# First attention of a two-layer block: four heads per group of value products, and a new order of the neighbouring work

## The chip, the cores and the metric

The kernel runs on one core of a Trainium2 chip. Its engines work side by side, each through its own list of instructions, and wait for each other on semaphores: TensorE (PE in the profile; PEld are its weight loads), VectorE (DVE), ScalarE (ACT), GpSimd (POOL) and SyncE (SP), which here issues most DMAs. The metric is the device time of one execution in microseconds (us), lower is better.

## What is computed

Two transformer layers over x of 32 sequences x 256 tokens x 128 channels, 16 heads of 8 channels, all float32 at the border. Cut to what the change touches, the first layer's attention:

```python
h = layernorm(x) * (1 + ca) + sa
Q, K, V = proj(Wq, bq), proj(Wk, bk), proj(Wv, bv)        # h @ W.T + b, split in 16 heads of 8
Qn = Q / maximum(norm(Q), 1e-12);  Kn = K / maximum(norm(K), 1e-12)
attn = softmax(Qn @ Kn.T / sqrt(8))                        # 256 x 256 per head and sequence
x = x + ga * ((attn @ V) * gate @ Wo.T + bo)
h = layernorm(x) * (1 + cb) + sb                           # goes to the first layer's experts
logits, depth = h @ gate_w + gate_b, h @ dp_w1 + dp_b1     # the router's products
```

After it come the four dense experts of layer 0, the causal attention of layer 1, and eight routed experts of layer 1.

## The kernel before

The program is a chain of phases with a barrier of all engines between them. The change lies in the first phase alone, in the functions named `dense` of each engine. They run over the 32 sequences (here: batches, `b`), one batch at a time, as a pipeline in which every engine works on several batches at once. No scheduler sets the order: each engine's loop over `b` is written out by hand, and an instruction starts when all ahead of it on its engine have started and its semaphores have come.

What belongs to batch b:

- `project` (PE): two products of 128 tokens each give Q, K and V in the PSUM tile `M` (`M[:,0]` for the first half of the tokens, `M[:,1]` for the second). `take` (DVE) adds the bias and stores them, one instruction for each half.
- `square` (ACT), `lengths` (DVE) and `lengths` (POOL, a Newton iteration of three rounds) give the inverse norms; `unit` (DVE) scales Q and K. `high` (ACT) and `low` (DVE) split them in float16 halves; four transposing DMAs on SP (`turned`) bring them to `qs3` and `ksd`.
- The 16 heads go in eight chunks `u` of two heads (CH = 8). `score` (PE) makes the 256 x 256 scores of both heads in a PSUM tile `SP[u % 2]`; `exp` (ACT) writes the exponentials to `pt[:, u % 4]`; `values` (PE) multiplies them with V. A head's V has 8 columns and a column of ones, padded to 32, so that a head uses 32 of the array's 128 columns: `tile_position=(0, 32 * g)` for head g of a group of four. The products are in float32, four instructions in a chunk (two halves of the keys, two heads).
- `tail_t(b, 0)` and `tail_t(b, 1)` (DVE) turn the first and the second half of `OP` into `oT`; `tail_n` divides by the sums and ends in `aT`; `tail_wo` (PE) multiplies with Wo; `tail_w`, `tail_g` and `tail_x` (DVE) add it to x; `tile_stats` and, every second batch, `variance` give the statistics of the next norm; `deviation` (POOL) finishes them for two batches.
- For the second norm: `normal` (ACT) writes z, `turn` (PE) transposes it into `M[:, 0]`, `enter` (ACT) modulates it into `hcur` and `h16`, `low` (POOL) makes the low half, `router` (PE) multiplies it into `M[:, 1]`, `extra` (DVE) takes that out of PSUM, `depth` (DVE) uses it.

In the loop for batch b PE issues score(b, u) and then values of two chunks earlier. Behind the chunks stand project(b + 3), both halves, at u = 1; tail_wo(b - 1) at u = 4; turn(b - 3) at u = 5; router(b - 3) at u = 7. ACT issues the eight exp, with high(b + 2) behind the third, square(b + 3) and normal(b - 3) behind the fifth, enter(b - 3) behind the seventh. The waits that matter below: exp(u) waits for score(u); score(u) for exp(u - 2), whose PSUM tile it writes; `take` for `project`, half by half; `lengths` (DVE) for `square`; `unit` for `lengths` of POOL; `high` for `unit`; `tail_w` for `tail_wo`; `project` for the `enter` and `extra` that emptied its half of `M` last.

## Time and profile before

| | us |
|---|---|
| median of 3 runs | 1810.16 (1807.91 to 1816.59) |
| the profiled execution | 1828.18 |
| its span | 1826.0 |
| PE busy over the span | 1556.5 (85%) |
| DVE busy | 1284.0 (70%) |
| ACT busy | 1188.8 (65%) |
| POOL busy | 882.6 (48%) |
| the stage of the change, from its first to its last exp | 81.4 to 524.5 |

The profiled execution is one run, some 18 us above the median; all rows below are from it. Starts are counted from the span's start. In the timeline a row is a run of like instructions of one engine: when it began, how long until its last record ends, the engine, the line of the kernel, output and inputs with their shapes, how many (x), and in brackets how long the engine had stood idle just before, with the instruction of another engine that ended the wait. Neighbouring instructions of one engine overlap by about a tenth of a microsecond, so that the distance of two starts, not the length of a row, is what a step costs its engine. One float32 product on PE stands as two records in the trace.

### The profile page before, as it was taken

What the parts mean: (1) busy time and instruction counts of PE and PEld (TensorE: products, weight loads), DVE (VectorE), ACT (ScalarE), POOL (GpSimd) and SP (SyncE); (2) the same over time, 40 slices, a digit from 0 to 9 for tenths busy, and PEclk for the clock granted to TensorE, in tenths of its full rate; (3) what the DMA queues carried; (4) which work ended last, traced back from release to release, by engine and by line L of the source; (5) the groups of instructions that cost most, each with busy time, mean ns of one, the idle gap of its engine ahead of it and who ended that gap; (6) DMA issues with size and microseconds to landing.
All of it is one profiled execution on the core that took longest, in us unless ns stands there. A gap on an engine that the chain in (4) does not pass through costs nothing.

```text
span 1826.0 us, 39932 instructions
## 1 busy us (share of the span) xinstructions
PE 1556.5 (85%) x12803; PEld 796.7 (44%) x12803; DVE 1284.0 (70%) x3451; ACT 1188.8 (65%) x2134; POOL 882.6 (48%) x1677
## 2 busy tenths in 40 slices
PE   5799999999967999779999999999999508989970
PEld 3334444444433444324444444444444306777750
DVE  6566777777747888836767677675877536777768
ACT  3777788778756989635565665556555517888860
POOL 6254544545511333324444438747465563555554
PEclk9899999999988999969999999999999558999995
DMA  5221112221208930022211213312221323222228
GB/s 155 75 45 36 36 36 41 42 37 36 47 13 331 386 125 1 23 57 50 48 41 41 46 38 66 69 43 66 45 62 43 112 77 97 75 77 76 76 66 258
DMA packets 238478, 141.20 MB, mean 77 GB/s; under 512 B 184163, under 2 KB 210659, under 8 KB 237253
## 3 DMA queue, kind: packets, MB, share of 16 engines
q1 hardware_dynamic: 227072, 119.72, 24.4%
q0 software_dynamic: 8640, 17.97, 3.0%
q8 instruction: 108, 1.77, 0.4%
q10 hardware_dynamic: 2564, 0.97, 0.2%
q14 instruction: 94, 0.76, 0.1%
HBM read 37.67 MB, written 58.98 MB: 53 GB/s over the span
## 4 chain that ended last, share of the span: by engine, by line
PE 42%; DVE 12%; issue 6%; ACT 2%; DVEq 2%; POOL 2%; DMA 1%; POOLq 1%; SPq 0%; ACTq 0%; another core or an unknown queue 0%
PE OP L2138 8%; PE OP L2003 5%; PE M L2101 5%; PE SP L1983 4%; DVE mx L1329 4%; PE SP L2298 3%; PE SP L2118 2%; PE M L2076 2%; PE M L2097 2%; PE M L2092 2%; PE OP L2313 2%; DVE pt L1620 2%; POOL h_dram L492 1%; PE OP L2150 1%; PE M L1993 1%
## 5 line engine op out<-in xcount | busy, mean ns | idle before, releaser
L863 ACT ACTIVATE pt<-SP 128x768 f32<-128x768 f32 x256 | 207.1, 809 | 250.4 <-PE SP L2118 236.4
L1329 DVE TENSOR_REDUCE mx<-M 128x2 f32<-128x512 f32 (+1 forms) x384 | 258.0, 683 | 104.5 <-PE M L2101 94.6
L531 POOL TENSOR_SCALAR_AFFINE_SELECT pt<-pt 128x256 f32<-128x256 f32 x512 | 198.6, 412 | 262.8 <-ACT pt L863 260.9
L750 ACT ACTIVATE pt<-SP 128x1024 f32<-128x1024 f32 x256 | 255.2, 1019 | 72.1 <-PE SP L1873 72.0
L562 POOL DMA_INDIRECT y_dram<-hT,dest x142 | 140.2, 987 | 134.2 <-DVE hT L1626 112.0
L964 ACT ACTIVATE pt<-SP,b 128x256 f16<-128x256 f32 x284 | 138.2, 487 | 81.8 <-PE SP L2298 81.2
L1892 PE MATMUL OP<-pt,vs 128*32 128x256 f32 x1408 | 186.5, 387 | 0.0
L492 POOL DMA_INDIRECT h_dram<-hT,slot x128 | 130.7, 1021 | 58.8 <-issue 31.7
L2138 PE MATMUL OP<-pt,vs 128*32 128x128 f32 (+1 forms) x1408 | 151.0, 338 | 4.7 <-POOL pt L531 4.7
L1620 DVE TENSOR_TENSOR pt<-vs,pt 128x256 f16<-128x256 f32 x284 | 115.7, 428 | 49.8 <-ACT vs L965 25.0
L656 POOL TENSOR_TENSOR st<-st,ksT 128x512 f32<-128x512 f32 x48 | 72.0, 1500 | 153.1 <-DVE ksT L1751 153.0
L965 ACT ACTIVATE vs<-SP,b 128x256 f32<-128x256 f32 x284 | 139.5, 491 | 0.0
L2298 PE MATMUL SP<-ksT,shared 128*128 128x256 f16 x852 | 129.6, 276 | 10.0 <-DVE ksT L1595 10.0
L2313 PE MATMUL OP<-shared,pt 128*128 x1704 | 130.6, 219 | 0.4 <-issue 0.2
L1734 DVE TENSOR_TENSOR pt<-vs,pt 128x512 f16<-128x512 f32 x128 | 104.7, 830 | 26.6 <-ACT vs L982 25.2
L577 POOL TENSOR_TENSOR nt<-rn 128x64 f32<-128x64 f32 x96 | 34.2, 357 | 166.3 <-DVE rn L1018 156.7
L2313 PEld LDWEIGHTS OP<-shared,pt 128*128 128x128 f16 x1704 | 107.1, 98 | 12.5 <-issue 0.8
L980 ACT ACTIVATE pt<-SP,b 128x512 f16<-128x512 f32 x128 | 88.0, 688 | 26.5 <-PE SP L1983 23.0
L2101 PE MATMUL M<-ksT,shared 24*128 24x128 f16 (+1 forms) x704 | 105.2, 250 | 0.0
L1873 PE MATMUL SP<-shared 32*128 32x256 f16 x1024 | 100.3, 274 | 3.6 <-ACT pt L750 3.5
L1892 PEld LDWEIGHTS OP<-pt,vs 128*32 128x32 f32 x1408 | 66.6, 109 | 72.0 <-ACT pt L750 19.6
L2138 PEld LDWEIGHTS OP<-pt,vs 128*32 128x32 f32 x1408 | 67.0, 110 | 69.5 <-issue 22.7
(325 smaller groups left out, 3344.9 us busy)
## 6 DMA issues: line engine op xcount, KB each, us to landing
h_dram<-shared SPq DMA_DIRECT2D x8, 4488.0 KB, 33.5
hT<-h_dram SPq DMA_DIRECT2D x71, 132.0 KB
rows<-g_dram SPq DMA_DIRECT2D x4, 2048.0 KB, 7.1
pt<-y_dram SPq DMA_DIRECT2D x32, 256.0 KB, 3.7
x_sb<-in_x SPq DMA_DIRECT2D x8, 512.0 KB, 8.8
pt<-in_w SPq DMA_DIRECT2D x4, 1024.0 KB
out<-x_sb SPq DMA_DIRECT2D x16, 256.0 KB, 3.0
shared<-st SPq DMA_TRANSPOSE x144, 2.4
```

Source lines behind the costliest of these rows:

```text
L492: pool.indirect_dma_start(out=h_dram, out_offset=bass.IndirectOffsetOnAxis(ap=slot[:, TT * b0 + t, k:k + 1], axis=0), in_=hrow[:, q % 2, t ...
L531: last = pool.affine_select(out=diag, in_=diag, compare_op=ALU.is_ge, fill=0.0, base=0, pattern=[[0, 2], [1, P]], channel_multiplier=-1)
L562: pool.indirect_dma_start(out=y_dram, out_offset=bass.IndirectOffsetOnAxis(ap=dest[:, g % XB, r:r + 1], axis=0), in_=ys[:, g % XB, r, :], ...
L750: act.activation(pt[:, u % 4], SP[u % 2][:], ACT.Exp, scale=SCALE).then_inc(s["exp"], 1)
L863: act.activation(pt[:, u % 4, :, 0:384], SP[u % 2][:, :, 0:384], ACT.Exp, scale=SCALE).then_inc(s["exp"], 1)
L1329: dve.tensor_reduce(to, M[:, k % 2, :].rearrange("p (j k) -> p j k", j=4 if k < 4 else 2), AX.X, ALU.max).then_inc(s["mred"], 1)
L1620: dve.tensor_tensor(hid1[:, g % 2, f, 1, :], relu[:, f, 0:BLK], hid1[:, g % 2, f, 0, :], ALU.subtract).then_inc(k["lo"], 1)
L1892: last = pe.matmul(OP[32 * g:32 * g + 32, j // 2, c:c + T], vsd[b % 3][:, k, HG * j + g, :], pt[:, u % 4, i, k * T:k * T + T], start=(k == ...
L2101: last = pe.matmul(v[:, n, :], qs3[b % 3][32 * g:32 * g + 3 * DH, j, q0:q0 + P], ks3[b % 3][32 * g:32 * g + 3 * DH, j, 0:kn], start=False, ...
L2138: last = pe.matmul(OP[32 * g:32 * g + 32, j // 2, c + q0:c + T], vs3[b % 3][:, k, HG * j + g, :], pt[:, u % 4, i, k * T:k * T + T - q0], s ...
L2298: last = pe.matmul(bank[f][:, 0:BLK], w16[1][:, 0, u, bass.ds(e * (F1 * P) + f * P, P)], hg[:, g % 2, v, :], start=(n == 0), stop=(n == 2))
L2313: last = pe.matmul(to[:, r, :], hid1[:, g % 2, f, v, r * P:(r + 1) * P], w16[1][:, 1, u, bass.ds(e * (F1 * P) + f * P, P)], start=False, s ...
```

## The change

Four things in the same phase:

1. `values(b, u)` for two heads becomes `values(b, j)` for the four heads of group j: eight instructions, each on another 32 columns than the one before it, behind every second score. It waits for the second of the group's two exponentials.
2. project(b + 3) is split: its first half goes behind score 2, its second behind score 4, ahead of tail_wo.
3. On DVE `take` comes ahead of `unit`; both halves of the tail (`tail_w`, `tail_g`) and `lengths` come ahead of `low`; `extra` comes behind `tail_n`. On ACT square and high stand together behind the sixth exp.
4. The second norm is run one batch later: normal, turn, enter for b - 4 in place of b - 3, router, `extra`, `depth` and POOL's `low` for b - 5. ACT's normal now stands behind the second exp and enter behind the eighth.

```diff
--- before.py
+++ after.py
@@ -636,15 +636,14 @@
                         deviation((b - 3) // 2)
                     if b + 2 < B:
                         place_v(b + 2)
-                    if b >= 4:
-                        low(b - 4)
+                    if b >= 5:
+                        low(b - 5)
                     if b + 3 < B:
                         lengths(b + 3)
                     if 1 <= b <= CHUNKS:
                         weight_low(b - 1)
-                low(B - 4)
                 deviation(B // 2 - 1)
-                for n in range(B - 3, B):
+                for n in range(B - 5, B):
                     low(n)
 
             def experts(l, E):
@@ -780,25 +779,25 @@
                 for b in range(B):
                     exp(b, 0)
                     exp(b, 1)
+                    if b >= 4:
+                        normal(b - 4)
                     exp(b, 2)
                     if b == 0:
                         sigmoid()
+                    exp(b, 3)
+                    exp(b, 4)
+                    exp(b, 5)
+                    if b + 3 < B:
+                        square(b + 3)
                     if b + 2 < B:
                         high(b + 2)
-                    exp(b, 3)
-                    exp(b, 4)
-                    if b + 3 < B:
-                        square(b + 3)
-                    if b >= 3:
-                        normal(b - 3)
-                    exp(b, 5)
                     exp(b, 6)
-                    if b >= 3:
-                        enter(b - 3)
                     exp(b, 7)
+                    if b >= 4:
+                        enter(b - 4)
                     if b < CHUNKS:
                         weight_high(0, b)
-                for n in range(B - 3, B):
+                for n in range(B - 4, B):
                     normal(n)
                     enter(n)
 
@@ -1271,30 +1270,29 @@
                 static_gate()
                 dve.drain()
                 for b in range(B):
-                    if b >= 4:
-                        extra(b - 4)
                     if b == 1:
                         dve.wait_ge(gate_in, 16 * HG)
                         dve.wait_ge(row_in, 16)
                     if b:
                         tail_t(b - 1, 1)
                         tail_n(b - 1)
+                    if b >= 5:
+                        extra(b - 5)
+                    if b + 3 < B:
+                        take(b + 3)
                     if b + 2 < B:
                         unit(b + 2)
-                    if b + 3 < B:
-                        take(b + 3)
                     if b:
                         tail_w(b - 1)
+                        tail_g(b - 1)
+                    if b + 3 < B:
+                        lengths(b + 3)
                     if b + 2 < B:
                         low(b + 2)
                     if b:
-                        tail_g(b - 1)
-                    if b + 3 < B:
-                        lengths(b + 3)
-                    if b:
                         tail_x(b - 1)
-                    if b >= 4:
-                        depth(b - 4)
+                    if b >= 5:
+                        depth(b - 5)
                     if b:
                         dve.drain()
                         tile_stats(TT * (b - 1), TT)
@@ -1309,7 +1307,7 @@
                 dve.drain()
                 tile_stats(NT - TT, TT)
                 variance(B // 2 - 1)
-                for n in range(B - 4, B):
+                for n in range(B - 5, B):
                     extra(n)
                     depth(n)
 
@@ -1854,8 +1852,8 @@
 
                     if b:
                         pe.wait_ge(s["qkv"], b)
-                    if b >= 7:
-                        pe.wait_ge(s["xin" if t else "h"], b - 6)
+                    if b >= 8:
+                        pe.wait_ge(s["xin" if t else "h"], b - 7)
                     pe.matmul(M[:, t, 0:3 * D], hT[:, b * T + t * P:b * T + (t + 1) * P], wqkv[0][:],
                               start=True, stop=True).then_inc(s["proj"], 1)
 
@@ -1875,26 +1873,24 @@
                                              start=True, stop=True, tile_position=(r0, 0))
                     last.then_inc(s["score"], 1)
 
-                def values(b, u):
-
-                    if u == 0:
+                def values(b, j):
+
+                    if j == 0:
                         pe.wait_ge(s["vs"], b + 1)
-                    pe.wait_ge(s["exp"], CH * b + u + 1)
-                    if b and u % 4 == 0:
-                        pe.wait_ge(s["o"], 2 * b + u // 4 - 1)
-                        if u:
+                    pe.wait_ge(s["exp"], CH * b + 2 * j + 2)
+                    if b and j % 2 == 0:
+                        pe.wait_ge(s["o"], 2 * b + j // 2 - 1)
+                        if j:
                             pe.wait_ge(s["wr"], b)
-                    j = u // 2
+                    c = (j % 2) * T
                     for k in range(TT):
-                        for i in range(2):
-                            g = 2 * (u % 2) + i
-                            c = (j % 2) * T
+                        for g in range(HG):
                             last = pe.matmul(OP[32 * g:32 * g + 32, j // 2, c:c + T],
                                              vsd[b % 3][:, k, HG * j + g, :],
-                                             pt[:, u % 4, i, k * T:k * T + T],
+                                             pt[:, 2 * (j % 2) + g // 2, g % 2, k * T:k * T + T],
                                              start=(k == 0), stop=(k == TT - 1),
                                              skip_group_check=True, tile_position=(0, 32 * g))
-                    last.then_inc(s["pv"], 1)
+                    last.then_inc(s["pv"], 2)
 
                 def tail_wo(b):
 
@@ -1908,7 +1904,7 @@
                 def turn(n):
 
                     pe.wait_ge(s["z"], n + 1)
-                    pe.wait_ge(s["qkv"], min(n + 7, B))
+                    pe.wait_ge(s["qkv"], min(n + 8, B))
                     if n:
                         pe.wait_ge(s["h"], n)
                     for t in range(TT):
@@ -1942,21 +1938,20 @@
                         score(b, u)
                         if b == 0 and u == 2:
                             pe.wait_ge(gl_in, 1)
-                        if CH * b + u >= 2:
-                            values((CH * b + u - 2) // CH, (u - 2) % CH)
-                        if u == 1 and b + 3 < B:
-                            for t in range(TT):
-                                project(b + 3, t)
+                        if u % 2 and CH * b + u >= 3:
+                            values((CH * b + u - 3) // CH, (u - 3) % CH // 2)
+                        if u == 2 and b >= 5:
+                            router(b - 5)
+                        if u in (2, 4) and b + 3 < B:
+                            project(b + 3, u // 2 - 1)
                         if u == 4 and b:
                             tail_wo(b - 1)
-                        if u == 5 and b >= 3:
-                            turn(b - 3)
-                        if u == 7 and b >= 3:
-                            router(b - 3)
-                values(B - 1, CH - 2)
-                values(B - 1, CH - 1)
+                        if u == 6 and b >= 4:
+                            turn(b - 4)
+                values(B - 1, NJ - 1)
                 tail_wo(B - 1)
-                for n in range(B - 3, B):
+                router(B - 5)
+                for n in range(B - 4, B):
                     turn(n)
                     router(n)
```

In the places below `shared`, `qkv`, `st` and `vs` are the buffers of Q, K, V and their halves, which alternate from batch to batch.

TensorE, one batch in the middle of the stage, before: every score (SP) is followed by the products of two heads (OP, x4).

```order
L1873 MATMUL SP<-shared 128x256 x4
L1892 MATMUL OP<-pt,vs 32x256 x4
L1859 MATMUL M<-wqkv,hT 128x384 x2
L1873 MATMUL SP<-shared 128x256 x4
L1892 MATMUL OP<-pt,shared 32x256 x4
L1873 MATMUL SP<-shared 128x256 x4
L1892 MATMUL OP<-pt,shared 32x256 x4
L1873 MATMUL SP<-shared 128x256 x4
L1892 MATMUL OP<-pt,shared 32x256 x4
L1904 MATMUL OP<-wo,aT 128x128 x2
L1873 MATMUL SP<-shared 128x256 x4
```

And the same stretch now:

```order
L1921 MATMUL M<-wx,hcur 128x68 x2
L1857 MATMUL M<-wqkv,hT 128x384
L1871 MATMUL SP<-shared 128x256 x4
L1888 MATMUL OP<-pt,vs 32x256 x8
L1871 MATMUL SP<-shared 128x256 x4
L1857 MATMUL M<-wqkv,hT 128x384
L1900 MATMUL OP<-wo,aT 128x128 x2
L1871 MATMUL SP<-shared 128x256 x4
L1888 MATMUL OP<-pt,vs 32x256 x8
L1871 MATMUL SP<-shared 128x256 x4
L1911 MATMUL M<-ident,z 128x128 x2
```

The products of values come half as often and twice as many at a time; the second half of the projection stands right ahead of the output projection.

VectorE, from the second turn of OP to the third part of the tail, before:

```order
L1181 STREAM_TRANSPOSE oT<-OP 128x512
L1186 RECIPROCAL rs<-oT 128x32
L1188 TENSOR_TENSOR rs<-rs,gateG 128x32
L1190 TENSOR_TENSOR an<-oT,rs 128x4x8x8
L1193 STREAM_TRANSPOSE aT<-an 128x256
L1165 TENSOR_TENSOR shared<-shared,rn 128x512
L1147 TENSOR_TENSOR qkv<-M,bqkv 128x3x128 x2
L1199 TENSOR_TENSOR ao<-OP,bo 128x256
L1174 TENSOR_TENSOR shared<-shared 128x64x8
L1174 TENSOR_TENSOR shared<-shared 128x32x16
L1204 TENSOR_TENSOR ao<-ao,rows 128x256
L1155 TENSOR_REDUCE n<-sq 128x64
```

And now:

```order
L1192 STREAM_TRANSPOSE aT<-an 128x256
L1228 TENSOR_TENSOR xt<-M,bx 128x136
L1146 TENSOR_TENSOR shared<-M,bqkv 128x3x128 x2
L1164 TENSOR_TENSOR qkv<-qkv,rn 128x512
L1198 TENSOR_TENSOR ao<-OP,bo 128x256
L1203 TENSOR_TENSOR ao<-ao,rows 128x256
L1154 TENSOR_REDUCE n<-sq 128x64
L1156 TENSOR_SCALAR n<-n 128x64
L1015 TENSOR_SCALAR rn<-n 128x64
L1017 TENSOR_SCALAR rn<-rn 128x64
L1173 TENSOR_TENSOR st<-qkv,st 128x64x8
L1173 TENSOR_TENSOR st<-qkv,st 128x32x16
```

The take of PSUM (M) moved ahead of the scaling (rn), the router's extra (xt) stands between aT and the take, and the low halves moved behind the lengths.

ScalarE, one batch, now (before, square stood alone behind the fifth and high behind the third exp):

```order
L758 ACTIVATE z<-x_sb,away,rstd 128x128 x2
L749 ACTIVATE pt<-SP 128x1024 x4
L730 ACTIVATE sq<-shared 128x512
L739 ACTIVATE st<-qkv 128x64x8
L740 ACTIVATE st<-qkv 128x32x16
L749 ACTIVATE pt<-SP 128x1024 x2
L769 ACTIVATE hT<-M,modT 128x256
L769 ACTIVATE hcur<-M,modT 128x256
```

Square and the high halves stand together behind the sixth exp, enter behind the eighth.

## Rows read from the trace of the kernel before

**Rows 1.** Table by stretches: PE, PEld, DVE, ACT, POOL busy; granted clock; DMA share, GB/s.

```profile
131.50:134.80 3.30, 3.30 (x20) 0.90 (x16) 0.87 (x3) 3.10 (x5) 2.26 (x8) 0.50 0.50 102
248.00:304.00 56.00, 54.53 (x443) 23.33 (x440) 41.36 (x121) 44.06 (x61) 27.82 (x82) 1.00 0.22 39
```

**Rows 2.** One line's instructions: the exponentials, durations in ns, first and last start.

```profile
L750 ACT ACTIVATE pt<-SP x256: 999/1023/1043, 81.4 to 524.5; 128x1024 f32<-128x1024 f32 x128
```

**Rows 3.** Timeline of PE in one batch.

```profile
300.66 0.71 PE L1904 MATMUL OP<-wo,aT 128*128 128x128 f32 x4
301.30 0.39 PE L1873 MATMUL SP<-shared 32*128 32x256 f16 x4
...
308.92 1.56 PE L1859 MATMUL M<-wqkv,hT 128*128 128x384 f32 x4
310.41 0.39 PE L1873 MATMUL SP<-shared 32*128 32x256 f16 x4
310.73 1.06 PE L1892 MATMUL OP<-pt,vs 128*32 128x256 f32 x8
311.72 0.39 PE L1873 MATMUL SP<-shared 32*128 32x256 f16 x4
```

**Rows 4.** Timeline of PE at the stage's end: the last two chunks of values.

```profile
525.45 1.18 PE L1892 MATMUL OP<-pt,vs 128*32 128x256 f32 x16
```

**Rows 5.** Timeline of ACT in the same batch as Rows 3.

```profile
301.28 0.63 ACT L731 ACTIVATE sq<-qkv 128x512 f32<-128x512 f32 x1
301.80 0.87 ACT L759 ACTIVATE z<-x_sb,away,rstd 128x128 f32<-128x128 f32 x2
302.57 1.98 ACT L750 ACTIVATE pt<-SP 128x1024 f32<-128x1024 f32 x2
304.44 0.56 ACT L770 ACTIVATE hT<-M,modT 128x256 f16<-128x256 f32 x1
...
305.34 1.03 ACT L750 ACTIVATE pt<-SP 128x1024 f32<-128x1024 f32 x1
...
310.85 1.02 ACT L750 ACTIVATE pt<-SP 128x1024 f32<-128x1024 f32 x1 [1.77 <-PE SP L1873]
312.35 0.63 ACT L740 ACTIVATE st<-qkv 128x512 f16<-128x512 f32 x1 [0.48 <-DVE qkv L1165]
...
313.40 1.92 ACT L750 ACTIVATE pt<-SP 128x1024 f32<-128x1024 f32 x2
```

**Rows 6.** Timeline of DVE over two batches, one with variance and one without.

```profile
287.12 0.42 DVE L1199 TENSOR_TENSOR ao<-OP,bo 128x256 f32<-128x256 f32 x1 [1.48 <-PE OP L1904]
...
295.36 0.72 DVE L1181 STREAM_TRANSPOSE oT<-OP 128x512 f32<-128x512 f32 x1 [0.84 <-PE OP L1892]
...
301.41 0.42 DVE L1199 TENSOR_TENSOR ao<-OP,bo 128x256 f32<-128x256 f32 x1 [2.09 <-PE OP L1904]
...
307.98 0.26 DVE L1229 TENSOR_TENSOR xt<-M,bx 128x136 f32<-128x136 f32 x1
309.04 0.72 DVE L1181 STREAM_TRANSPOSE oT<-OP 128x512 f32<-128x512 f32 x1 [0.80 <-PE OP L1892]
...
311.44 0.87 DVE L1165 TENSOR_TENSOR qkv<-qkv,rn 128x512 f32<-128x512 f32 x1
312.23 1.01 DVE L1147 TENSOR_TENSOR shared<-M,bqkv 128x384 f32<-128x384 f32 x2
315.09 0.43 DVE L1199 TENSOR_TENSOR ao<-OP,bo 128x256 f32<-128x256 f32 x1 [1.84 <-PE OP L1904]
```

**Rows 7.** Timeline of ACT behind the last batch.

```profile
538.04 0.88 ACT L759 ACTIVATE z<-x_sb,away,rstd 128x128 f32<-128x128 f32 x2 [6.87 <-POOL away L608]
```

**Rows 8.** Timeline of POOL: the Newton rounds of lengths, and what follows them.

```profile
305.83 0.50 POOL L577 TENSOR_TENSOR nt<-rn 128x64 f32<-128x64 f32 x1 [2.65 <-DVE rn L1018]
...
311.15 0.61 POOL L598 TENSOR_TENSOR vs<-qkv,ones 128x256 f32<-128x256 f32 x1
```

**Rows 9.** Timeline of PE early in the stage: a wait.

```profile
130.47 0.44 PE L1915 MATMUL M<-ident,z 128*128 128x128 f32 x2 [2.23 <-ACT z L759]
```

## The prediction

> **What bounds the kernel now.** I read first the table by stretches, for the middle of the stage. Of 56 us PE is busy 54.5, ACT 44.1, DVE 41.4, POOL 27.8, at a granted clock of 1.00, which is 2.4 GHz [rows 1]: PE bounds it, and the three others have slack. The line of the exponentials gives the stage's length: 256 of them from 81.4 to 524.5, so 443.1 us, about 13.9 us a batch [rows 2]. The timelines of one batch say the same from below. Behind `project` PE goes score, values, score without a hole (310.41, 310.73, 311.72), and ACT meanwhile waits 1.77 us for a score that stands behind `project` [rows 3, 5]. DVE waits twice a batch: for `tail_wo` (2.09, 1.84) and for the last values before `tail_t` (0.84, 0.80) [rows 6]. So a cheaper PE helps at once, until ACT or DVE, or the hand-overs between them, take its place. That new bound is what has to be worked out.
>
> **What four heads at once are worth.** A block of two heads costs PE 311.72 - 310.73 = 0.99 us, eight blocks a batch. Does a block of four heads cost twice that? Two products of `project` (384 columns, whole array) take 310.41 - 308.92 = 1.49 us, 0.745 each, so by proportion a product of 256 columns takes 0.50 alone and the four of a block 1.99 one behind the other; they take 0.99, so two heads already run side by side [rows 3]. At the stage's end the last two chunks of values stand in a row with no score between them: 16 records in a row of 1.18 us, where 8 take 1.06 [rows 3, 4]. The second two heads cost 0.12 us, which is partly the wait for the last exp. So four heads run side by side, and a block of four costs 1.0 us, as two do now. Removed are four blocks of 0.99, PE's work falls by 3.95 us a batch, from 13.7 (a batch without a wait of PE) to 9.7. Bounds: 0.9 (nothing for the second pair) and 1.98 (nothing shared); I take 1.0, since the row of 16 is the same operation on the same tiles.
>
> A rule speaks against it. In the rows a float32 product is two records, and a block of two heads, 8 records, takes four steps of about 0.22 us. The Trainium skill (TensorE: Matmul & The Clock Gate, Part 3, The mechanism) says that matmuls start and end strictly in program order. Then the second record of a head would hold back the next head, and eight products would take nine steps in place of four. The 16 records in 1.18 us do not agree with that rule; it stands as a rival below.
>
> **ACT, batch by batch.** Its steps, start to start [rows 5]: two exp 304.44 - 302.57 = 1.87, so eight take 7.5; square 0.52; normal 0.77; enter 305.34 - 304.44 = 0.90; high 313.40 - 312.35 = 1.05. Together 10.7 us, if it never waits. Its work is only reordered.
>
> **DVE.** From one `tail_w` to the next it takes 301.41 - 287.12 = 14.29 us with variance and 315.09 - 301.41 = 13.68 without; less the two waits of each (0.84 and 2.09; 0.80 and 1.84) that is 11.36 and 11.04, mean 11.2 us of work with drains [rows 6]. Nothing of it goes away. PE falls to 9.7, so DVE is the fullest engine, and each wait on it counts in full from then on.
>
> **The new order of DVE, followed once round.** Time 0 is the start of `tail_t(b-1, 1)`. `tail_n` is issued by 311.44 - 309.04 = 2.40; then `extra` (0.26, ends 2.66). PE's second half of `project` waits for exactly this `extra`, since that emptied its half of M; PE has been through its other work by then (9.7 against more than 12). One half of `project` is about 0.8 long, so it lands at 3.5. DVE has meanwhile taken the first half (0.5 of the 1.01 for both) and stands at 3.1: **a new wait of 0.5**, where there was none. take ends at 4.1, `unit` (0.6 to 0.8) at 4.8; `tail_wo` has followed `project` at once (0.64, ends 4.2), so `tail_w` does not wait: the old wait of 2 us is gone. `tail_w` and `tail_g` bring DVE to 5.6, where `lengths` needs `square`. That stands behind the sixth exp; its score stands behind `tail_wo` on PE: score from 4.1, exp 0.44 later (310.85 - 310.41) at 4.5, square at 5.5, done at 6.2. **A second new wait of 0.6.** Then `lengths`, `low`, `tail_x`, `depth`, statistics and `tail_t(b, 0)` fill the rest without a wait: high is done at 7.2, before DVE comes to `low`. The ring closes after 11.2 + 0.5 + 0.6 = **12.3 us**, and does so only if the values of the last group are there: ACT reaches exp 7 at 8.0, so the values end at about 10.6, before 12.3. The old wait of 0.8 is gone as well. Per batch: 13.9 to 12.3.
>
> **Who is moved past, and who waits behind.** `tail_wo` now stands behind the half of `project` that waits for `extra`, and behind both score 5 and so ACT: ACT is idle some 1.6 us there, which costs nothing while DVE is the ring. Values for four heads wait for the second exp and hold back score u + 1: it comes 1.0 us later at most, while ACT still has one exp (0.94) in hand; 0.1 to 0.2 a time, in ACT's slack. POOL: its Newton rounds take 311.15 - 305.83 = 5.3 us, their result is needed by `unit` of the next batch, about 9 us after `lengths` of DVE; deviation, placing of V and low are some 7 us more every second batch, which still ends before the next rounds (5.3 + 7 in a ring of 12.3) [rows 8]. This is nothing, but with no cover left in the odd batches. The four transposing DMAs of `turned` start later in the batch by some 2 us; their scores come two batches later. Nothing.
>
> **The ends.** The 25 batches 4 to 28 take 12.3 each, 308 us. The first four have no second norm, but two of `weight_high`, about 1.3 us, on ACT: 11.6 each, 46 us. Of the last three, without projections and lengths, I take 10.5, 9.4 and 8.2 (to the last exp), near ACT's sum without what they lack. Together 382 against 443.1: 61 us less. Behind the last batch one more second norm is open. Normal of batch 30 started at 538.04, right behind the last deviation of POOL [rows 7]; now POOL's `low(27)` stands behind that deviation, and enter(29) behind `low(27)`, ahead of normal(30): 1.6 us more. Net 59. I take 57, as the early batches have waits of their own (2.23 us of PE at 130 us [rows 9]) of which I can't tell that all go.
>
> **The sum.** The profiled execution took 1828.2 us: 1771 after. Its distance to the median, 18 us, is not the stage's matter, so 57 us comes off the median: 1810.2 - 57 = **1753 us**.
>
> **Rivals.**
> - *The new waits shrink* (0.10). If `project` and square come earlier than I have it, the ring is DVE's 11.2: 25 x 1.1 = 28 us less, 1726. Against it: both waits hang on `extra` and on score 5, which are in DVE's own ring.
> - *More waits* (0.18). POOL's odd batches, or a `project` that finds PE in a block of values (1.0 us), add up to 0.9 a batch: 13.2, 25 x 0.9 = 22 us more, 1775. For it: POOL has no slack there.
> - *Heads one behind the other, in program order* (0.05). By steps: nine of 0.22 plus 0.1 in place of 0.99 twice, 2.08 a group; PE stays at 13.7 + 4 x 0.1 = 14.1 against 13.9 now. The waits of the tail and of ACT at `project` don't matter then: 1810 to 1818, no change. Only rows 4 speak against it, but plainly. It is the rule of the skill above.
> - *The clock falls* (0.05), the one that ends slower. PE is now idle for some 2.6 of 12.3 us. Early in the stage it waited 2.23 us, and the 3.3 us behind that ran at a granted clock of 0.50, 1.2 GHz, in which PE was busy throughout [rows 1, 9]. At that level PE's 9.7 us of work double. PE's work at a share f of low clock is 9.7 (1 + f); with the two hand-overs of 0.5 and 0.6 and about 1 us of waits for exp it reaches 13.9 at f = 0.2 if all of that adds up, at 0.4 if nothing does. From there on the change costs time; at f = 0.6 it is 15.5 + 0.5, 2 us a batch, 1810 + 60 = 1870. Against it: no single gap that I find is over about 1 us, and a PE kept waiting longer is also busier at low clock, which brings the clock back.
> - Something that no row shows in either direction (0.04).
>
> **Chances.** Forecast 0.58, 1740 to 1766 (0.5 us a batch either way). The range takes in the second rival in full and nearly all of the first: 1728 to 1784, with 0.15 outside. Faster by over 0.5% (about what a measurement of this kernel tells from no change): 0.58 + 0.10 + 0.18 + 0.02 = 0.88; within 0.5%: 0.06; slower: 0.06.
>
> **What would show it.** PE's row of values: x16 in a block, some 1.1 long, 1.0 to the next start; two different starts 2 us long would mean the third rival. DVE's timeline: idle ahead of the second take of M, ended by PE M, and ahead of the reduce of sq, ended by ACT sq, about 0.5 each, and none ahead of `tail_w` and `tail_t`. First to last exp: 382 us. Granted clock 1.00 in the stage. If DVE instead waits for POOL's rn or ACT for z, the second rival is at work; if DVE is idle more than 1.5 us a batch, my ring is wrong.

## The result

The changed kernel takes 1761.6 us in the median (1749.0 to 1769.4, 4 runs), the kernel before 1813.4 us in the same comparison (1807.9 to 1820.1): ratio 0.971, 95% interval 0.965 to 0.976, 52 us less. 1753 had been forecast, 57 us less, with a range of 1728 to 1784.

The profiled executions lie 70 us apart (1828.2 and 1758.0), of which the phase of the change has 54: it ends, where the next phase's first VectorE instruction starts, at 545.6 us before and at 491.9 after. The other 16 us lie in phases that the change does not touch. The medians say 52; the rest of this text goes by the changed phase alone.

Page of the changed kernel, parts 1 and 5 (busy us, share of the span, instructions; then groups with busy time, mean ns of one, idle time before and what ended it):

```profile
span 1755.9 us, 39931 instructions
PE 1454.9 (83%) x12803; PEld 760.9 (43%) x12803; DVE 1273.9 (73%) x3451; ACT 1180.9 (67%) x2134; POOL 887.6 (51%) x1677
...
L749 ACT ACTIVATE pt<-SP 128x1024 f32<-128x1024 f32 x256 | 251.5, 1035 | 51.4 <-PE SP L1871 51.1
```

All five engines have as many instructions as before, within a record or two. PE is busy 1454.9 us in place of 1556.5: the same products, more of them side by side. The line of the exponentials, which answers to [rows 2]:

```profile
L749 ACT ACTIVATE pt<-SP x256: 1006/1024/1084, 80.0 to 468.6; 128x1024 f32<-128x1024 f32 x128
```

From first to last exp it is 388.6 us in place of 443.1. In the table by stretches (PE, PEld, DVE, ACT, POOL busy, granted clock, DMA) PE is no longer the fullest engine, where in [rows 1] it had 54.5 of 56 us. The first stretch shows a granted clock well under 1; over the whole stage, from first to last exp, its mean is 0.93, and 0.99 in the kernel before:

```profile
80.00:136.00 56.00, 46.24 (x422) 17.78 (x422) 34.59 (x87) 45.07 (x59) 24.16 (x67) 0.79 0.18 36
...
304.00:360.00 56.00, 45.02 (x501) 20.57 (x502) 46.65 (x139) 50.33 (x71) 33.62 (x96) 1.00 0.23 47
```

By this table ACT is the busiest engine (50.33 of 56 us), ahead of DVE (46.65). Busy time leaves out the drains on DVE and the gaps between its small instructions; counted from start to start, as in the prediction, a batch of 12.04 us holds 11.1 us of DVE's work and 10.7 us of ACT's, as the waits below show.

PE's timeline in the middle of the stage, answering to [rows 3]:

```profile
299.87 0.61 PE L1900 MATMUL OP<-wo,aT 128*128 128x128 f32 x4
300.41 0.39 PE L1871 MATMUL SP<-shared 32*128 32x256 f16 x4
300.73 1.07 PE L1888 MATMUL OP<-pt,shared 128*32 128x256 f32 x16
301.73 0.39 PE L1871 MATMUL SP<-shared 32*128 32x256 f16 x4
...
304.48 0.39 PE L1871 MATMUL SP<-shared 32*128 32x256 f16 x4 [0.66 <-ACT pt L749]
305.30 0.39 PE L1871 MATMUL SP<-shared 32*128 32x256 f16 x4 [0.43 <-ACT pt L749]
...
310.72 0.88 PE L1857 MATMUL M<-wqkv,hT 128*128 128x384 f32 x2 [0.27 <-DVE xt L1228]
...
323.24 0.88 PE L1857 MATMUL M<-wqkv,hT 128*128 128x384 f32 x2 [1.16 <-DVE xt L1228]
```

The block of four heads has 16 records, lasts 1.07 and costs 301.73 - 300.73 = 1.00 us, what the block of two cost. PE now waits for ACT (0.66 and 0.43 in these rows), and for `extra` (xt) ahead of the second half of the projection, 1.16 us in every second batch and 0.27 in the others. DVE in the same stretch, answering to [rows 6]:

```profile
300.07 0.56 DVE L1146 TENSOR_TENSOR qkv<-M,bqkv 128x384 f32<-128x384 f32 x1 [0.60 <-PE M L1857]
...
302.42 0.69 DVE L1154 TENSOR_REDUCE n<-sq 128x64 f32<-128x512 f32 x1 [0.34 <-ACT sq L730]
...
307.22 1.30 DVE L1180 STREAM_TRANSPOSE oT<-OP 128x512 f32<-128x512 f32 x2
...
311.64 0.56 DVE L1146 TENSOR_TENSOR shared<-M,bqkv 128x384 f32<-128x384 f32 x1 [0.60 <-PE M L1857]
...
324.16 0.56 DVE L1146 TENSOR_TENSOR qkv<-M,bqkv 128x384 f32<-128x384 f32 x1 [0.60 <-PE M L1857]
```

The two waits of [rows 6], for `tail_wo` and for the last values, are gone (both turns of OP stand in one row without a wait). The two that the prediction named are there, 0.60 ahead of the second take and 0.34 ahead of `lengths`. From one such take to the next it is 11.57 and 12.52 us, in the mean 12.04; less the two waits that is 11.1 us of work. ACT waits for the score of its sixth exp, 1.79 and 0.89 in turn, 1.34 in the mean, which leaves 10.7 us of work:

```profile
300.84 1.02 ACT L749 ACTIVATE pt<-SP 128x1024 f32<-128x1024 f32 x1 [1.79 <-PE SP L1871]
...
312.41 1.02 ACT L749 ACTIVATE pt<-SP 128x1024 f32<-128x1024 f32 x1 [0.89 <-PE SP L1871]
```

### The profile page after: what moved, and what is told of

It is laid out like the page before. It is cut to its first block, busy times and chain, and to the rows that moved or that the text cites. A ratio compares the mean times of both kernels' runs of the same rounds, so it can differ in the third digit from the quotient of the medians.

```text
span 1755.9 us, 39931 instructions
## 1 busy us (share of the span) xinstructions
PE 1454.9 (83%) x12803; PEld 760.9 (43%) x12803; DVE 1273.9 (73%) x3451; ACT 1180.9 (67%) x2134; POOL 887.6 (51%) x1677
## 4 chain that ended last, share of the span: by engine, by line
PE 49%; DVE 11%; issue 4%; POOL 3%; DVEq 2%; ACT 1%; DMA 1%; POOLq 1%; SPq 0%; ACTq 0%
PE OP L2133 8%; PE OP L2308 6%; PE SP L2293 5%; DVE mx L1327 5%; PE OP L1998 5%; PE SP L1978 5%; PE M L2096 4%; PE M L2071 3%; PE SP L2113 2%; PE M L2087 2%; PE M L2092 2%; POOL h_dram L492 2%; PE OP L2145 1%; PE M L1988 1%; PE M L2283 1%
## 5 line engine op out<-in xcount | busy, mean ns | idle before, releaser
L749 ACT ACTIVATE pt<-SP 128x1024 f32<-128x1024 f32 x256 | 251.5, 1035 | 51.4 <-PE SP L1871 51.1
L1888 PE MATMUL OP<-pt,vs 128*32 128x256 f32 x1408 | 98.6, 399 | 0.3 <-ACT pt L749 0.3
L2133 PEld LDWEIGHTS OP<-pt,vs 128*32 128x32 f32 x1408 | 67.6, 111 | 71.1 <-issue 24.0
L1978 PE MATMUL SP<-hT,w 128*128 128x512 f16 x384 | 95.0, 384 | 0.0
```

The source lines that it names most:

```text
L749: act.activation(pt[:, u % 4], SP[u % 2][:], ACT.Exp, scale=SCALE).then_inc(s["exp"], 1)
L1978: last = pe.matmul(bank[k % 4].rearrange("p (n t) -> p n t", t=T), w16[l][:, 0, u, k * P:(k + 1) * P], h16[:, v, bass.ts(g, TT), :], start ...
L2133: last = pe.matmul(OP[32 * g:32 * g + 32, j // 2, c + q0:c + T], vs3[b % 3][:, k, HG * j + g, :], pt[:, u % 4, i, k * T:k * T + T - q0], s ...
```

## Experiments

Twelve runs: eleven further kernels, and the changed one once more. They stood on three chips, and the kernel before has another median on each, so a kernel's time is only to be read beside its own:

- before at 1841.6: values in fours alone; new order alone; extra early; extra and square early.
- before at 1819.3: changed with scores repeated, with load on DVE, with load on ACT, head by head.
- before at 1843.4: values in fours with scores repeated; both early with six and with three scores repeated; changed, again.

"Ratio" is estimated from all fast runs of both kernels, with its 95% interval, and can differ by some thousandths from the quotient of the medians. "Stage" is the distance from the first to the last exp's start in the kernel's profile, one profile for each kernel; "full clock" is a batch, from its first exp to the next batch's, in the middle of the stage, in batches whose granted clock was 1.00 throughout.

| kernel | median, us | ratio to before | stage, us | batch at full clock, us |
|---|---|---|---|---|
| before | 1813.4 | | 443.1 | 13.7 to 14.4 |
| changed | 1761.6 | 0.971 (0.965 to 0.976) | 388.6 | 12.04 |
| values in fours alone | 1818.8 | 0.989 (0.982 to 0.996) | 427.6 | |
| the same, scores repeated | 1810.2 (one run) | | 419.6 | 13.1 |
| new order alone | 1841.4 | 1.000 (0.996 to 1.004) | 444.5 | 14.2 |
| changed, extra early | 1781.3 | 0.970 (0.963 to 0.976) | 388.3 | 11.5 |
| changed, extra and square early | 1773.2 | 0.962 (0.955 to 0.970) | 372.9 | 11.2 |
| changed, scores repeated | 1754.4 | 0.967 (0.961 to 0.974) | 377.2 | 12.06 |
| changed, load on DVE | 1760.5 (one run) | | 388.5 | 12.04 |
| changed, load on ACT | 1759.2 (one run) | | 391.7 | 12.05 |
| changed, head by head | 1755.1 (one run) | | 386.5 | 12.04 |
| both early, six scores repeated | 1757.6 | 0.953 (0.949 to 0.957) | 363.0 | 11.3 |
| both early, three scores repeated | 1752.0 | 0.951 (0.946 to 0.956) | 356.3 | 11.2 |
| changed, again | 1782.3 | 0.968 (0.963 to 0.973) | 386.5 | 12.05 |

### Which part of the change gives the gain

Values in fours alone, in the kernel before (cut: the loop of PE; `values` itself is that of the changed kernel):

```diff
-                        if CH * b + u >= 2:
-                            values((CH * b + u - 2) // CH, (u - 2) % CH)
+                        if u % 2 and CH * b + u >= 3:
+                            values((CH * b + u - 3) // CH, (u - 3) % CH // 2)
```

> The kernel before with one part of the change: values for four heads at once; every other order is the old one. My theory (the four-head blocks open the door, the new order sets how far one gets): PE falls to 9.7 us a batch, and a ring through ACT takes over: exp 7, values, both turns of OP, tail_n, unit, high behind the third exp, and the exps up to the next exp 7. By the rows it is ACT's 10.7 us plus a wait of 1.9 us ahead of high, about 12.6 us a batch; first to last exp 405 us against 443 before and 389 after, the kernel 35 to 42 us faster than before. Rival (the order is only along for the ride): the same 12.0 us a batch as the full change, 389 us. Rival (the four-head blocks are nothing alone): 435 us or more.

Measured: 427.6 us, none of the expected values. The block of four heads alone takes 15.5 us off the stage, the whole change 54.5. In the kernel's time the gain is small, a ratio of 0.989 with an interval that ends at 0.996. Its table by stretches shows one reason why the 405 were missed:

```profile
304.00:360.00 56.00, 46.60 (x448) 20.19 (x452) 41.34 (x122) 44.71 (x62) 27.91 (x82) 0.82 0.22 39
```

PE had less to do than before and waited more, and the granted clock of this stretch is 0.82, in the mean of the stage 0.84. A block of values took 1.94 us where the clock was low, 1.07 where it was not:

```profile
345.21 1.07 PE L1890 MATMUL OP<-pt,vs 128*32 128x256 f32 x16
347.51 0.44 PE L1913 MATMUL M<-ident,z 128*128 128x128 f32 x2 [1.23 <-ACT z L759]
347.88 1.15 PE L1873 MATMUL SP<-shared 32*128 32x256 f16 x8
348.96 1.94 PE L1890 MATMUL OP<-pt,vs 128*32 128x256 f32 x16
```

The same kernel with redundant work on PE, to tell the effect of the clock from that of the order. The scores of chunks 4 and 5 are computed four times, by this in `score`:

```diff
-                    for k in range(TT):
+                    again = {4: 3, 5: 3}.get(u, 0)
+                    for k in [0, 1] * (again + 1):
```

> The run with values in fours alone (old order), and redundant scores where PE waits there: chunks 4 and 5 four times, 1.3 us of PE a batch. It took 427.6 us at granted clocks of 0.82 to 0.88; its batches with the least of low clock took 12.95. If its order alone, at full clock, makes a batch 12.7 to 13.0 us (ACT waits for unit ahead of high): all batches so, 398 to 406 us in all, and the new order is worth about 0.9 us a batch. If the clock does not matter there: 427 us or more.

Measured: 419.6 us, between the two expected outcomes. The clock came up (0.88 to 1.00 by stretches of 56 us) but not all the way. Its batches at full clock lie between 12.5 and 13.6, mean 13.1, a little over the expected 12.7 to 13.0. So the stage missed the 398 to 406 on both counts. Against 12.04 the new order is worth 1.0 us a batch at full clock; over the stage that is some 25 to 30 of the 39 us between 427.6 and 388.6. That the rest is the clock (mean 0.84 against 0.93) is argued, not shown. ACT waits in this kernel where the expectation had it wait, for the scaling ahead of high:

```profile
272.97 0.63 ACT L740 ACTIVATE st<-qkv 128x512 f16<-128x512 f32 x1 [0.86 <-DVE qkv L1165]
```

but only 0.2 to 0.9 us, not 1.9, and 1.20 for a score behind `project`. Which of these waits sets the 13.1 us no run here shows.

The new order alone, in the changed kernel, with values in twos behind every score (cut: the loop of PE; `values` itself is that of the kernel before):

```diff
-                        if u % 2 and CH * b + u >= 3:
-                            values((CH * b + u - 3) // CH, (u - 3) % CH // 2)
+                        if CH * b + u >= 2:
+                            values((CH * b + u - 2) // CH, (u - 2) % CH)
```

> The changed kernel with values in twos again, behind every score; all of the new order is kept. My theory: PE is the bound as before with its 13.3 to 13.9 us a batch, DVE's two new waits lie in its slack, and the first to the last exp takes 435 to 445 us; the kernel within 0.5% of the one before. Rival (the order is the gain): 400 us or less. Third possibility: the new hand-over, project waiting for extra, holds up the bounding PE, and the stage is longer than before, 450 us or more.

Measured: 444.5 us, ratio 1.000, as expected. DVE's wait ahead of the second take is there and large, and in every second batch PE, the bound, waits for a turn of OP, the `tail_t` that frees its tile. First the row of DVE, then that of PE:

```profile
300.73 0.56 DVE L1146 TENSOR_TENSOR qkv<-M,bqkv 128x384 f32<-128x384 f32 x1 [2.84 <-PE M L1857]
```

```profile
323.26 1.06 PE L1890 MATMUL OP<-pt,shared 128*32 128x256 f32 x8 [1.39 <-DVE oT L1180]
```

Its batches take 13.5 and 14.9 in turn, so the new waits lie in DVE's slack in one batch of two only. In the stage the order alone is worth nothing, and with the four-head blocks it is worth 1 us a batch: it is an order for a kernel that PE does not bound.

### Whether the ring through DVE sets the batch

"Ring" here is one turn through DVE's instructions of a batch, with the waits in it. One instruction more on DVE, 0.29 us long and needed by nobody, between `tail_g` and `lengths` (in this and the next cut the line that declares the tile `load` is left out):

```diff
+                    dve.tensor_scalar(load[:], ident[:].unsqueeze(1).to_broadcast([P, 2, P]), 2.0, None, ALU.mult)
```

> The changed kernel with one more instruction a batch on VectorE, 128 x 256 float32 between tail_g and lengths, some 0.3 to 0.4 us, that nobody needs. Its place is right ahead of the wait for square (0.34). If the ring through DVE is what sets a batch: the instruction first fills that wait, and the batches at full clock go from 12.04 to between 12.05 and 12.15 us in the mean; the wait for square is gone from DVE's waits. If DVE's sum of work alone counted, with no part of the wait given back: 12.4.

Measured: 12.04, a hair under the expected 12.05 to 12.15, and no wait for square is left:

```profile
299.73 0.42 DVE L1204 TENSOR_TENSOR ao<-ao,rows 128x256 f32<-128x256 f32 x1
300.07 0.29 DVE L1289 TENSOR_SCALAR load<-ident 128x256 f32<-128x256 f32 x1
300.49 0.69 DVE L1155 TENSOR_REDUCE n<-sq 128x64 f32<-128x512 f32 x1
```

From the start of `tail_g` to that of `lengths` it is 300.49 - 299.73 = 0.76 us, where the changed kernel has 0.77: the instruction filled the wait and no more.

One instruction more on ACT, behind the third exp:

```diff
+                    act.activation(load[:], ident[:].unsqueeze(1).to_broadcast([P, 2, P]), ACT.Copy)
```

> The changed kernel with one more instruction a batch on ScalarE, 128 x 256 float32 behind the third exp, 0.3 to 0.45 us, that nobody needs. ACT has 0.9 to 1.8 us of idle time behind it, ahead of exp 5. If DVE's ring sets the batch: 12.04 us a batch at full clock, within 0.1, and the wait of ACT for score 5 shorter by what was added. Rival (ACT's 10.7 us of work and its hand-overs set it): 12.4 us.

Measured: 12.05; ACT's wait for score 5 is 0.69 and 1.51 where the changed kernel has 0.89 and 1.79. The instruction lasts 0.46 us, the next one starts 0.31 us behind it, and 0.20 and 0.28 of that came out of the wait. So ACT does not set the batch.

Both loads say only what costs nothing. That the waits on DVE cost something is shown by taking them away. `extra` moved ahead of `tail_n`:

```diff
                         tail_t(b - 1, 1)
-                        tail_n(b - 1)
                     if b >= 5:
                         extra(b - 5)
+                    if b:
+                        tail_n(b - 1)
```

> The changed kernel with one line of VectorE moved: extra between the second turn of OP and tail_n, about 1.7 us earlier in the batch. My theory: the ring of the changed kernel is extra, second half of project, take. Then DVE's wait of 0.60 ahead of the second take goes, and PE's wait for xt (up to 1.16 in odd batches) with it, since project starts as soon as PE comes to it; 12.04 us a batch at full clock fall to 11.45 to 11.6, first to last exp 373 to 378 us in place of 389, the kernel 10 to 15 us faster than the changed one. Rival (ACT or POOL sets the 12.04): no change.

Measured: at full clock 11.27 and 11.77, mean 11.52, as expected: the two takes stand in one row, without a wait between them.

```profile
323.38 0.98 DVE L1146 TENSOR_TENSOR qkv<-M,bqkv 128x384 f32<-128x384 f32 x2
326.17 0.69 DVE L1154 TENSOR_REDUCE n<-sq 128x64 f32<-128x512 f32 x1 [0.35 <-ACT sq L730]
```

But the stage is 388.3 us, as long as the changed kernel's, and the expected 373 to 378 were missed; nor is the kernel's time the expected 10 to 15 us better (ratio 0.970). Seven batches behind the first five met low clock and took 12.8 to 14.4 us in place of 11.3 and 11.8; in the changed kernel it is five, the sixth among them. The mean granted clock of the stage is 0.91, in the changed kernel 0.93. What the order won, the clock took back.

With square ahead of the sixth exp as well:

```diff
                     exp(b, 3)
                     exp(b, 4)
-                    exp(b, 5)
                     if b + 3 < B:
                         square(b + 3)
+                    exp(b, 5)
```

> As the run with extra moved, and square ahead of the sixth exp, in the hole in which ACT waits for score 5. My theory: the wait of 0.34 of DVE for square goes too, if the take is done by then; 11.2 to 11.3 us a batch, which is DVE's work alone, first to last exp 366 to 372 us. Rival: square now waits for the take itself and holds up exp 5 by some tenths, and nothing or less is gained over the run with extra alone.

Measured: 11.33 and 11.09 in turn, mean 11.21, as expected. DVE's wait for square is gone; a wait of 0.23 for `project` ahead of the second take is left in every second batch. Square itself now waits 0.65 and 0.40 for the take, as the rival had it, and that costs the batch nothing, since ACT has slack. The stage is 372.9, just over the 366 to 372, with eight batches of 12.5 to 14.2 at a lowered clock behind the first.

### What the clock costs

The changed kernel with redundant scores, `again = {0: 1, 1: 1, 2: 1, 7: 3}`: those of chunks 0, 1 and 2 twice, those of chunk 7 four times.

> The changed kernel with redundant work on TensorE: the scores of chunks 0, 1 and 2 are computed twice, those of chunk 7 four times, right behind each other into the same place, so that PE is busy where it waits now. By the rows that is 6 x 0.22 = 1.3 us a batch more, in PE's waits. What is tested is the clock: in the changed kernel's trace the stage has the granted clock 0.79 in its first 56 us, and the batches with 3 to 7 us at half clock take 12.8 to 14.4 us where the others alternate between 11.6 and 12.5. If the waits of PE bring the clock down and that costs those batches their time, the clock stays at 1.00 now, all batches take 11.6 to 12.6, and first to last exp is 375 to 382 us in place of 389, although PE has more to do. Rival (the early batches are slow for a reason of their own, and PE's work counts): 389 us or more.

Measured: 377.2 us, within the expected range, 11.4 us less than the changed kernel although PE has some 1.3 us a batch more to do (the estimate of the expectation). The four near copies of the changed kernel that the other runs hold (load on DVE, load on ACT, head by head, and itself again) have stages of 386.5 to 391.7, so the difference is 9 to 15 us. The granted clock in the stretches that stood at 0.79 and 0.91:

```profile
80.00:136.00 56.00, 50.04 (x610) 23.87 (x612) 39.39 (x96) 50.67 (x67) 26.87 (x69) 0.97 0.27 41
136.00:192.00 56.00, 50.00 (x606) 25.15 (x602) 47.05 (x140) 49.67 (x70) 34.66 (x99) 1.00 0.25 48
```

The second to fifth batches take 11.3, 11.3, 11.3 and 11.0 in place of 12.0, 14.2, 14.0 and 13.5. In the middle of the stage PE's waits for ACT have shrunk to 0.21 and 0.22, and the long one for `extra` is still there:

```profile
306.63 0.61 PE L1872 MATMUL SP<-shared 32*128 32x256 f16 x8 [0.21 <-ACT pt L749]
...
308.46 0.61 PE L1872 MATMUL SP<-shared 32*128 32x256 f16 x8 [0.22 <-ACT pt L749]
...
312.95 0.88 PE L1857 MATMUL M<-wqkv,hT 128*128 128x384 f32 x2 [0.94 <-DVE xt L1228]
```

In the kernel's time the gain is not shown: its ratio is 0.967, that of the changed kernel 0.971 and 0.968, within each other's intervals. The gain is read from the profiles, one of each kernel.

Extra and square early together with the redundant scores, first the same six, then three (`{0: 1, 1: 1, 7: 1}`), beside the changed kernel itself:

> The run with extra and square moved, and the redundant scores of before on top (chunks 0, 1 and 2 twice, chunk 7 four times, 1.3 us of PE a batch). Without them that kernel took 11.21 us a batch at full clock, but 12.5 to 14.2 in the eight batches that met the low clock, and 372.9 us from first to last exp. If only the clock kept it from its 11.2: all batches 11.0 to 11.5, first to last exp 350 to 356 us, the kernel 30 to 36 us faster than the changed one. If PE, with 9.7 + 1.3 = 11.0 us of work a batch, is now in the way: 11.5 to 11.9 a batch and 360 us or more.

> As the run before, with half of the redundant work: chunks 0, 1 and 7 twice, 0.65 us of PE a batch. If the clock stays up with it, 11.1 to 11.3 a batch and 348 to 354 us, a little better than with six; if the clock needs more, some batches of 12.5 and more are left and the stage is between 354 and 373 us.

> The changed kernel itself, unaltered, on the same chip as the three others, for the comparison with them. 12.04 us a batch where the clock is full, some low stretches, 385 to 392 us from first to last exp; all theories say the same.

Measured: 363.0, 356.3 and 386.5 us. With six repeats the batches take 11.3, as in the first of the two outcomes, but the stage is 363.0, as in the second, and the kernel 25 us faster than the changed one, not 30 to 36. That is still 10 us of stage less than without repeats (372.9), and 7 more than with three. With three the batch is 11.2 and the stage 2 us over the range of the first outcome, at the lower edge of the second: the first batch (12.5) and the thirtieth (12.0) met low clock, and the sixth took 12.7 at full clock. By the medians this kernel is the fastest of those on its chip, though its runs overlap with those of six repeats: 1752.0 us (1748.7 to 1760.1) beside 1782.3 (1778.6 to 1788.9) of the changed kernel, 30 us less, and no run of the one reaches the other.

### Whether products start in program order

The eight products of a block, head by head:

```diff
-                    for k in range(TT):
-                        for g in range(HG):
+                    for g in range(HG):
+                        for k in range(TT):
```

> The changed kernel with the eight products of a block in another order: both key halves of head 0, then both of head 1, and so on, in place of all four heads' first halves and then all four heads' second halves. Four records of the same 32 columns now follow each other in the program. If matmuls start strictly in program order, hardly two heads overlap and a block takes 13 steps of 0.22 us, near 3 us in place of 1.0; the stage is over 500 us long. If TensorE lets work on other columns pass, as the 16 records in 1.18 us at the stage's end suggest, the block stays near 1.0 us; if it can hold back only a few records, it lies between, 1.2 to 2 us.

Measured: the block is as long as in the changed kernel, and so is the stage (386.5 us).

```profile
300.49 0.39 PE L1871 MATMUL SP<-shared 32*128 32x256 f16 x4
300.81 1.09 PE L1888 MATMUL OP<-pt,shared 128*32 128x256 f32 x16
```

In the program four records of one head stand ahead of the next head's first, and still all four heads are done in 1.09 us; 13 steps of 0.22 us, one head behind the other, would be near 3. The rule of the Trainium skill (TensorE: Matmul & The Clock Gate, Part 3, The mechanism), by which matmuls start and end strictly in program order, does not agree with this trace.

## Why the prediction was right, and where it was off

**Four heads at once.** Predicted 1.0 us a block from the row of 16 records, measured 1.00. The rival with heads one behind the other is out, by this measurement and by the run head by head.

**The ring of DVE.** Predicted 12.3 us: 11.2 of work, waits of 0.5 and 0.6. Measured 12.04 at full clock: 11.1 of work, waits of 0.60 and 0.34. That these waits sit in the ring is shown: without the first a batch is 11.52, without both 11.21, of which 0.23 in every second batch is still a wait, so again 11.1 of work. The old waits for `tail_wo` and the last values went, as forecast. Score 5 came when the prediction had it, 311.98 - 310.57 = 1.41 us behind the end of `extra` (forecast 4.1 - 2.66 = 1.44). The wait for square was sized at 0.6 for two smaller reasons: from that score to the end of square it took 1.97 us in place of 2.1, and DVE came to `lengths` 3.07 us behind the end of `extra` in place of 2.94, mostly because its first wait was 0.60 and not 0.5.

**ACT and POOL** had slack, as said. ACT took an instruction of 0.46 us more a batch without a longer batch. POOL had been given no cover in the odd batches; it has some. Ahead of its Newton rounds it waits for DVE's `lengths`, 0.77 us in one batch and 4.02 in the next, and DVE does not wait for the inverse norms in the middle of the stage:

```profile
304.43 0.58 POOL L577 TENSOR_TENSOR nt<-rn 128x64 f32<-128x64 f32 x1 [0.77 <-DVE rn L1017]
...
315.66 0.58 POOL L577 TENSOR_TENSOR nt<-rn 128x64 f32<-128x64 f32 x1 [4.02 <-DVE rn L1017]
```

**The ends.** Predicted 46, measured 52.5 us for the first four batches, and 46.5 with the clock held up by repeated scores; predicted 28, measured 30.1 for the last three; predicted 308, measured 306 for the 25 between. Behind the last exp it is 491.85 - 468.59 = 23.3 us, before 545.61 - 524.50 = 21.1: 2.2 us more where 1.6 were forecast. The order of waits is the one named: `low(27)` (POOL's hT) behind the last deviation, enter(29) behind that, and normal(30) last:

```profile
483.26 0.56 ACT L769 ACTIVATE hT<-M,modT 128x256 f16<-128x256 f32 x1 [5.85 <-POOL hT L613]
483.73 0.56 ACT L769 ACTIVATE hcur<-M,modT 128x256 f32<-128x256 f32 x1
484.18 0.87 ACT L758 ACTIVATE z<-x_sb,away,rstd 128x128 f32<-128x128 f32 x2
```

**The clock.** This is the step that the prediction got wrong. It stands there with a chance of 0.05, as a case of its own that ends slower, because no single wait seemed to be over about 1 us; and a granted clock of 1.00 in the stage was named as a sign of being right. It came in part, inside the forecast case, and cost a part of the gain. From the third batch to the fourth PE waits 1.17, 0.43 and 0.74 us, and the clock falls with the last of these waits:

```profile
119.55 0.61 PE L1871 MATMUL SP<-shared 32*128 32x256 f16 x4 [0.74 <-ACT pt L749]
120.08 1.65 PE L1857 MATMUL M<-wqkv,hT 128*128 128x384 f32 x2
121.66 0.61 PE L1871 MATMUL SP<-shared 32*128 32x256 f16 x4
122.20 1.94 PE L1888 MATMUL OP<-pt,vs 128*32 128x256 f32 x16
...
126.85 1.07 PE L1888 MATMUL OP<-pt,vs 128*32 128x256 f32 x16
```

```profile
119.00:126.00 7.00, 6.45 (x33) 2.34 (x34) 3.75 (x11) 4.37 (x5) 4.91 (x16) 0.51 0.26 58
```

At a granted clock of 0.51 the block of values takes 1.94 us in place of 1.07 and half a projection 1.65 in place of 0.88. PE, which at full clock has a fifth of its time to spare (busy 45.02 of 56 us), is the bound again for that while. The prediction's price for it was fair: it had a batch back at 13.9 us when 0.2 to 0.4 of PE's work is done at low clock, and the third and fourth batch, with a mean clock of 0.76, so low for about half their time, took 14.2 and 14.0. That the clock would come back by itself was right too; it fell again. In the stage it cost about 11 us (388.6 against 377.2 with the clock held up).

**Why the sum came out close.** 382 us had been forecast for the stage, 388.6 were measured. The batches at full clock were 0.26 us shorter than forecast, some 6.5 us over the 25 between, and the clock took about 11. Two errors of opposite sign met, so part of the closeness is luck. The stage gave 54.5 us of the 61 worked out for it (the forecast of 57 had taken 2 off for waits of the early batches), 2.2 were lost behind it, and 52 are left, as the medians say. (That the medians agree to the microsecond is chance: the runs spread over 12 and 20 us.)

**Still open.** Which of PE's waits bring the clock down and which don't. In the changed kernel's middle PE waits 0.66, 0.43 and 0.43 us a batch for ACT, and 1.16 or 0.27 for `extra`, and most batches keep full clock. With `extra` early the wait of 1.16 is gone, those for ACT are the same, and the clock fell more often. With scores repeated the wait for `extra` is there (0.94), those for ACT are at most 0.22 in the middle of the stage, and the clock stayed at 1.00 from the second batch to the last. That points at the waits for ACT and not at the longest one; no run here changes them alone.

## What to carry to other kernels

When the bounding engine gets cheaper, follow the next fullest engine once round a period and add each of its waits: the period was its work plus two hand-overs, and moving one function each removed nearly all of both. Count the engine's work from start to start: by busy time another engine looked fuller. An order tuned for one bound can be worth nothing under another, so measure an order together with what it was made for. And after a cut of work on TensorE look at the granted clock of every stretch, not only at the mean: time won by less work was partly lost to half clock, and with 0.65 us of redundant products a batch (an estimate) the stage was 17 us shorter than without them (356.3 against 372.9).

## What the runs showed of the hardware

- Float32 products of four heads, each on its own 32 columns of the array, run side by side and cost what those of two do (1.00 us). They do so in either program order: 16 records last 1.07 us with the heads in turn and 1.09 with four records of one head ahead of the next head's first.
- TensorE's granted clock fell to its lower level (0.50, 1.2 GHz) again and again behind waits of 0.43 to 1.17 us (mean 0.93 over the stage), and with some 1.3 us of redundant products a batch in those waits it stayed at 1.00 from the second batch to the last. A batch that met the low clock took up to 3 us more (14.4 in place of 11.3, with `extra` early).
- A kernel with less waiting was not safe from it: `extra` early has a shorter batch than the changed kernel at full clock (11.52 against 12.04), a lower mean clock (0.91 against 0.93) and the same stage (388.3 against 388.6).
